# Routing weights spread by transfers from DRAM instead of by a selector product on TensorE

## What is computed

```
shared = silu(h @ Ws_up) @ Ws_down
biased = h @ centroids.T + expert_biases         # 64 experts; the 8 largest are chosen
w      = sigmoid of the 8 chosen affinities, divided by (their sum + 1e-8)
cw     = zeros(T, 64); cw[token, chosen] += w    # routing weights
y      = silu(h @ W_up[e]) @ W_down[e]           # 64 experts of 64 hidden units
x      = x + gb * (shared + sum over e of cw[:, e] * y[e])
```

## Time and profile before

| | us |
|---|---|
| median of 3 runs | 1983.4 |
| lowest, highest | 1980.77, 1983.73 |
| span of the profiled execution | 1978.2 |
| PE busy in the span | 1579.2 (80%) |
| DVE busy | 1410.5 (71%) |
| ACT busy | 1163.7 (59%) |
| POOL busy | 998.2 (50%) |

### The profile page before, as it was taken

How to read it: one execution, slowest core, us unless ns; L and a number is a source line. 1 busy time by engine, 2 the same in 40 slices (tenths; PEclk the granted TensorE clock), 3 DMA queues, 4 the chain that set the end, 5 groups by cost and what they waited for, 6 DMA issues and landing times. The chain is left out here.

```text
span 1978.2 us, 32338 instructions
## 1 busy us (share of the span) xinstructions
PE 1579.2 (80%) x9101; PEld 752.0 (38%) x9101; DVE 1410.5 (71%) x2630; ACT 1163.7 (59%) x1991; POOL 998.2 (50%) x923
## 2 busy tenths in 40 slices
PE   3599989898988889945764677777664999999998
PEld 2245444444444445422442122222222444444443
DVE  5677868686868687827766988898998555555554
ACT  1177766666667677625544444443333777777776
POOL 4144535353535353425862455544441667777776
PEclk7699989998999999976887777777777999999999
DMA  4332212131313131000003000000000000000000
GB/s 104 92 100 58 85 50 85 46 89 39 96 36 99 36 99 41 22 1 0 1 0 86 0 1 0 0 0 0 0 0 0 1 6 6 5 5 5 0 6 11
DMA packets 51217, 64.95 MB, mean 33 GB/s; under 512 B 7980, under 2 KB 42440, under 8 KB 51080
## 3 DMA queue, kind: packets, MB, share of 16 engines
q1 hardware_dynamic: 49640, 61.12, 10.8%
q10 hardware_dynamic: 1440, 2.10, 0.3%
HBM read 34.36 MB, written 28.05 MB: 32 GB/s over the span
## 5 line engine op out<-in xcount | busy, mean ns | idle before, releaser
L804 DVE TENSOR_REDUCE bmax<-p1b 128x4 f32<-128x512 f32 x640 | 408.5, 681 | 117.4 <-PE p1b L621 110.6
L553 ACT ACTIVATE pT<-p2b 128x512 f32<-128x512 f32 x640 | 373.2, 595 | 173.5 <-PE p2b L636 172.2
L1618 POOL TENSOR_TENSOR hid_l<-e_hid,hid_h 128x512 f16<-128x512 f32 x264 | 305.4, 1160 | 139.3 <-ACT hid_h L1758 138.2
L619 PE MATMUL p1b<-ks,qs 96*128 96x512 bf16 (+3 forms) x1024 | 274.0, 314 | 59.4 <-DVE bmax L804 33.0
L1864 DVE TENSOR_TENSOR e_hid<-act_u,e_cb 128x512 f32<-128x512 f32 x256 | 174.8, 687 | 187.6 <-ACT act_u L1772 163.5
L530 POOL TENSOR_SCALAR_AFFINE_SELECT pT<-pT 128x1280 f32<-128x1280 f32 (+2 forms) x192 | 162.3, 876 | 241.5 <-ACT pT L553 241.5
L636 PE MATMUL p2b<-qs,ks 96*128 96x512 bf16 (+3 forms) x1024 | 253.5, 310 | 7.3 <-ACT pT L553 6.7
L1772 ACT ACTIVATE act_u<-ub 128x512 f32<-128x512 f32 x264 | 157.3, 596 | 83.6 <-PE ub L1672 82.4
L621 PE MATMUL p1b<-causal,identb 128*128 128x128 bf16 x1024 | 200.1, 227 | 0.0
L649 PE MATMUL ob<-pT,vs 128*32 128x512 f32 (+3 forms) x2048 | 196.1, 456 | 2.2 <-POOL pT L530 2.2
L1479 DVE TENSOR_TENSOR_SCAN hs<-dA,dBx 128x512 f32<-128x512 f32 x128 | 183.3, 1432 | 17.0 <-ACT dA L1385 11.0
(11 more groups left out here) (254 smaller groups left out, 3027.5 us busy)
## 6 DMA issues: line engine op xcount, KB each, us to landing
qs<-q_stacks SPq DMA_DIRECT2D x64, 204.0 KB
q_stacks<-parts SPq DMA_DIRECT2D x96, 128.0 KB
k_stacks<-parts SPq DMA_DIRECT2D x96, 128.0 KB
ks<-k_stacks SPq DMA_DIRECT2D x64, 192.0 KB
qs<-nparts SPq DMA_DIRECT2D x192, 4.0 KB
out_dram<-x_tok SPq DMA_DIRECT2D x8, 256.0 KB, 2.3
wmod<-L_wmod SPq DMA_DIRECT2D x2, 384.0 KB, 5.8
q_stacks<-zeros SPq DMA_DIRECT2D x4, 192.0 KB, 3.1
```

Source lines behind the costliest of these rows:

```text
L553: act.activation(pT[:, g2 % 2, v, :], p2b[v % 2][:, :], ACT.Exp, scale=SCALE).then_inc(exp_done, 1)
L619: pe.matmul(bank[:, at * P:(at + c + 1) * P], qs[:, slot, m, c * P:(c + 1) * P], ks[:, slot, m, 0:(c + 1) * P], start=True, stop=False, sk ...
L804: dve.tensor_reduce(to, src, AX, ALU.max).then_inc(first_read, 1)
L1618: pool.tensor_tensor(hid_l[:, place(T), :], hid[:, place(T), :], hid_h[:, place(T), :], ALU.subtract).then_inc(split_ready, 1)
```

## The change

The selector and its matmul go. Once a batch the turned weights (64 x 512, f32, scaled by 64 on ACT) are stored to a DRAM tensor `shares`. For every slot SP then issues two transfers; each reads one row of 512 weights and writes it to 64 partitions of a tile of the ring `share` (eight tiles of 128x512 f32 in SBUF). DVE multiplies `act_u` with that tile. SP waits for `hid_ready` of the slot eight before, so that the tile is free. With the product go the two halves of the weights and what formed them: `double`, `high` and `split` become one activation `scaled_shares`, and the transpose reads `rest` itself. SP's program, which only stored the output before, is now a loop over rounds and slots. `share`, the function, is called `divide`.

```diff
-        pick = sb("e_pick", [P, ET, 2], FP16)
-        sel = sb("sel_e", [P, ET, P], FP16)
-        cw = sb("cw", [P, TILES, 2, E])
-        parts = sb("cw_parts", [P, 2, S], FP16)
-        low = sb("cw_low", [P, S])
+        turned_shares = sb("turned_shares", [E, S])
+        share = sb("share", [P, SHARES, S])
...
-            with sp.Fori(0, B) as r:
-                sp.wait_ge(x_ready, r + 2)
-                sp.dma_start(out[r, :, :].rearrange("(i p) d -> p i d", p=P), k.x[:, bass.ds(r * TILES, TILES), :]).then_inc(stored, 16)
+            def step(r, pre, main, post):
+
+                def save():
+                    b = r + 1
+                    sp.wait_ge(shares_ready, b + 2)
+                    sp.dma_start(shares_dram[b, :, :], turned_shares[:, :]).then_inc(shares_saved, 16)
...
+                if main:
+                    sp.wait_ge(shares_saved, (r + 1) * 16)
+                    for T in range(ET):
+                        before = T - SHARES if T >= SHARES else T - SHARES + ET - SLOTS
+                        if T >= SHARES or post:
+                            sp.wait_ge(hid_ready, r * SLOTS + before + 1 + RING)
+                        for a in range(2):
+                            sp.dma_start(share[a * EF:(a + 1) * EF, T % SHARES, :],
+                                         shares_dram[r, 2 * T + a, :].partition_broadcast(EF)).then_inc(share_loaded[T % SHARES], 16)
+                        if post and T == DOWN_LAG + SHARES + 4:
+                            store()
+                        if pre and T == ET - 2:
+                            save()
...
                 def turn_weights():
+                    pe.wait_ge(loaded, LOADS)
                     pe.wait_ge(cw_ready, b + 1)
                     for c in range(TILES):
-                        mm = pe.transpose(preb[:, c * P:(c + 1) * P], cw[:, c, :, :].rearrange("p a e -> p (a e)"), k.ident[:, :])
+                        mm = pe.transpose(preb[0:E, c * P:(c + 1) * P], rest[:, c, :], k.ident[:, :])
...
                 if main:
-                    pe.wait_ge(parts_ready, r + 3)
                     pe.wait_ge(hT_split, r + 1)
...
-                        if T < ET:
-                            pe.wait_ge(hid_ready, free(q, T, bank))
-                            pe.matmul(cb[bank(T)][:, :], sel[:, T, :], parts[:, r % 2, :], start=True, stop=True).then_inc(c_done, 1)
...
-                def high():
+                def scaled_shares():
                     act.wait_ge(cwT_done, b + 2)
-                    act.wait_ge(parts_ready, b + 2)
-                    act.activation(parts[:, b % 2, :], preb[:, :], ACT.Copy).then_inc(high_ready, 1)
+                    if main:
+                        act.wait_ge(shares_saved, b * 16)
+                    act.activation(turned_shares[:, :], preb[0:E, :], ACT.Copy, scale=W_SCALE).then_inc(shares_ready, 1)
...
                         if T < ET:
-                            dve.wait_ge(c_done, r * ET + T + 1)
-                            dve.tensor_tensor(hid[:, place(T), :], act_u[:, bank(T), :], cb[bank(T)][:, :], ALU.mult).then_inc(hid_ready, 1)
+                            dve.wait_ge(share_loaded[T % SHARES], (r * USES + T // SHARES + 1) * 32)
+                            dve.tensor_tensor(hid[:, place(T), :], act_u[:, bank(T), :], share[:, T % SHARES, :], ALU.mult).then_inc(hid_ready, 1)
```

More of the change, by code:

```diff
@@ L1515, in experts @@
     DOWN_LAG = 3
-    LOW = 2.0 ** 11
+    SHARES = 8
+    USES = ET // SHARES
+    shares_dram = nc.dram_tensor("shares", [B, E, S], F32).ap()
     with ExitStack() as ctx:
@@ L1547, in experts @@
         ub = [ps(f"ub{i}") for i in range(2)]
[L1548 removed]
         yb, preb, routeb, postb = ps("e_yb"), ps("e_preb"), ps("routeb"), ps("e_postb")
[L1550 removed]
+        share_loaded = [sem(f"share_loaded{s}") for s in range(SHARES)]
+        shares_saved = sem("shares_saved")
         cent_psum, cent_ready = sem("cent_psum"), sem("cent_ready")
[L1552 to L1554 removed]
+        xn_ready, xT_done, hT_ready, aff_done, sig_ready, cw_ready, cwT_done, shares_ready = (
+            sem("e_" + n) for n in ("xn_ready", "xT_done", "hT_ready", "aff_done", "sig_ready", "cw_ready", "cwT_done", "shares_ready"))
         biased_ready, top_ready, gate_ready = sem("biased_ready"), sem("top_ready"), sem("gate_ready")
[L1556 to L1557 removed]
+        u_done, silu_ready, hid_ready, hid_rounded, split_ready, down_done, yg_ready, turned, x_ready, hT_split = (
+            sem("e_" + n) for n in ("u_done", "silu_ready", "hid_ready", "hid_rounded", "split_ready", "down_done", "yg_ready",
                                     "turned", "x_ready", "hT_split"))
@@ L1561, in experts @@
         block = ctx.enter_context(nc.Block())
-        CREDITS = {silu_ready: RING, hid_ready: RING, split_ready: RING, down_done: RING, yg_ready: 1, turned: 1, x_ready: 1, parts_ready: 2, low_read: 1,
+        CREDITS = {silu_ready: RING, hid_ready: RING, split_ready: RING, down_done: RING, yg_ready: 1, turned: 1, x_ready: 1, shares_ready: 1,
                    biased_ready: 1, top_ready: 1, aff_done: 1, cwT_done: 1}
@@ L1590, in _, with store @@
         def _(sp):
-            with sp.Fori(0, B) as r:
-                sp.wait_ge(x_ready, r + 2)
-                sp.dma_start(out[r, :, :].rearrange("(i p) d -> p i d", p=P), k.x[:, bass.ds(r * TILES, TILES), :]).then_inc(stored, 16)
+            def step(r, pre, main, post):
[3 more added lines that the diff above has]
+                    sp.dma_start(shares_dram[b, :, :], turned_shares[:, :]).then_inc(shares_saved, 16)
+                def store():
+                    sp.wait_ge(x_ready, r + 1)
+                    sp.dma_start(out[r - 1, :, :].rearrange("(i p) d -> p i d", p=P), k.x[:, bass.ds((r - 1) * TILES, TILES), :]).then_inc(stored, 16)
+                if main:
[11 more added lines that the diff above has]
+                            save()
+                elif pre:
+                    save()
+                else:
+                    store()
+            rounds(sp, step)
             sp.wait_ge(stored, B * 16)
@@ L1599, in _ @@
                 pool.sem_inc(s, n)
[L1600 to L1607, removed]
             def step(r, pre, main, post):
@@ L1777, in step @@
                         if pre:
-                            for at, f in ((4, pre_h), (10, sigmoid), (21, high)):
+                            for at, f in ((4, pre_h), (10, sigmoid), (21, scaled_shares)):
                                 if T == at:
@@ L1781, in step @@
                 elif pre:
-                    pre_h(), sigmoid(), high()
+                    pre_h(), sigmoid(), scaled_shares()
                 else:
@@ L1818, in strike @@
                 def strike():
-                    dve.wait_ge(loaded, LOADS)
+                    dve.wait_ge(cwT_done, b + 1)
                     dve.wait_ge(top_ready, b + 2)
+                    dve.sem_inc(passed, 1)
                     for c in range(TILES):
@@ L1835, in total, with divide @@
                     link(dve.reciprocal(wsum[:, :], wsum[:, :]))
[L1837 to L1842, removed]
-                steps = ((0, pre_norm), (9, bias), (10, largest), (11, strike), (12, mask), (13, chosen), (14, total), (15, share), (16, double))
-                def split():
-                    dve.wait_ge(high_ready, b + 1)
-                    lo = parts[E:2 * E, b % 2, :]
-                    dve.tensor_tensor(low[E:2 * E, :], preb[E:2 * E, :], lo, ALU.subtract).then_inc(low_read, 1)
-                    dve.wait_ge(low_read, b + 2)
-                    dve.tensor_scalar(lo, low[E:2 * E, :], LOW, None, ALU.mult).then_inc(parts_ready, 1)
+                def divide():
+                    dve.tensor_tensor(rest[:, :, :], rest[:, :, :], wsum[:, :].unsqueeze(2).broadcast_to([P, TILES, E]), ALU.mult).then_inc(cw_ready, 1)
+                steps = ((0, pre_norm), (9, bias), (10, largest), (11, strike), (12, mask), (13, chosen), (14, total), (15, divide))
                 def residual():
@@ L1869, in step @@
                         if pre:
-                            for at, f in (*steps, (21, split)):
+                            for at, f in steps:
                                 if T == at:
```

10 lines of the change are left out of this document (2 added, 8 removed).

## The result

The changed kernel takes **1998.0 us** (median of four executions, 1994.5 to 2001.2). The kernel before, on the same chips, takes 1982.1 (four executions, 1978.8 to 1983.7). The ratio is 1.0089, with an interval of 1.007 to 1.0107: the change costs some 16 us. The profiled span grew from 1978.2 to 1996.7, by 18.5 us.

The account below looks back on a forecast made before the run. TensorE bounded the old kernel (1.51 us a slot); GpSimd and VectorE in turns (1.56) the new. Span 1978.2 + 7.7 (rounds) + 1.9 (start) + 1.6 (end) = 1989, plus 5.2 to the median: 1994 us, range 1970 to 2035.

Parts of the forecast that it names:

- rival C: Expert slots: full lengths of product and subtraction exclude each other, 1.85 us a slot, about 2067 us; chance 0.06.
- term (a): Start of a round: each normalisation waits its turn, products 1 to 3 come late, turns resume 1.2 us late.
- term (b): ScalarE's switch to sigmoid and back, some 4.3 us, partly filled by turns and hT: 0.8 us lost a round.
- term (c): Routing steps in a round push GpSimd a slot ahead, costing 0.5 us.
- B: Expert slots: exclusion hardly bites, ScalarE bounds at 1.22 us a slot, round 49 us, about 1935 us; chance 0.09.
- G: Rounds: turns rule but the gaps nearly vanish, round 53.9 us, total 1974 us; chance 0.10.
- D: SP and transfers too slow, VectorE waits for every pair: 2076 us, mild form 2000 to 2030; chance 0.08.
- E: TensorE's gaps of 0.3 us per slot bring its clock to 1.2 GHz, 2.6 us a slot; chance 0.02.
- (1): VectorE's product: mean well over 0.69 us, about 1.4, since it stands in its turn, never under.
- (4): Rounds between gated results take 56 to 57 us.
- (5): TensorE is busy about 10 points less, its clock still 1.00.
- (6): VectorE's waits on share transfers are near zero save in round 0.

Follow-up runs that it names:

- e1: Changed kernel with its transfers, but VectorE's product reads a constant PSUM tile instead of the share tile (routing weights left out): 1947.3 us, ratio 0.9832.
- e3: Kernel before with its seven matmuls, no transfers, but the product reads a constant SBUF tile instead of bank e_cb (weights left out): 2012.4 us, ratio 1.0156.
- e4: Changed kernel with silu's result act_u in the two freed PSUM banks, complete computation: 1946.1 us, ratio 0.982.
- e2: Changed kernel without the save, loads and waits of the weights; share tiles filled once with ones: 1996.0 us, ratio 1.0064.
- e5: Changed kernel with VectorE's strike halved after slots 11 and 12, mask to divide a slot later: 1994.3 us, ratio 1.0079.
- e7: The unaltered changed kernel timed again, as reference beside the halved strike: 1999.1 us, ratio 1.0102.

## Why the prediction was right

The forecast was 1994, in a range of 1970 to 2035, with "slower" at 0.66; it came out at 1998.0, slower. Its likeliest case is the one that happened, and e1, e3 and e4 show its cause.

**The slot.** 0.54 + 1.02 = 1.56 us from three pairs of the earlier trace rows; measured 1.56 (0.56 + 1.00). The sum is right to the hundredth because its two parts are off by 0.02 in opposite ways (the earlier trace rows themselves give 0.55 for the first). The full lengths (rival C, 1.85) are refuted in nearly every slot. The Trainium skill (SBUF — State Buffer, section "SBUF: two separate sides") says that whoever starts first holds the port pair for the whole instruction. The turns agree with it; "the whole instruction" does not, since in each turn some 0.14 us of the instruction lies beside the other's (0.69 less 0.56, 1.16 less 1.00). Which part of the instruction that is, as "before the first read" in the prediction, no row shows.

**The gaps of a round** were the term that was mis-sized. A round took 57.6, not 56.5. The forecast's gaps beyond the turns were 2.5 us, and 3.7 came. Its terms can be held against the ends of the products. Slots 0 to 5: six turns, 0.8 for the normalisations and term (a) make 11.4; measured 11.44. Slots 10 and 11, across ScalarE's switch: two turns, 1.0 for hT and term (b) make 4.9; measured 4.99. Slots 12 to 18: seven turns, 0.8 for the routing operations and term (c), 0.5 us for "the routing steps push GpSimd a slot ahead", make 12.2; measured 13.3. So term (c) was 1.1 us a round too small. The missing time first shows at the strike, behind which the product ended 2.69 after the one before and not 1.56, since GpSimd was 0.03 us ahead. With another order of turns e2 gets back 0.8 of it and e5 0.6. The table under e4 adds what the forecast does not say. Against the kernel before, the 0.05 us per slot matters little (0.2 in slots 20 to 32, and slots 0 to 10 even take 0.7 less). The round is 2.2 us longer because slots 11 to 19, where VectorE's routing steps join the turns, take 2.7 us more.

**The parts of the sum.** Up to the first gated result I had 1.9 for the start and 1.1 for round 0, 3.0; measured 4.4. The wait for the first transfer was right within 0.3 (2.2). What I left out is that TensorE, having stood, is at the low clock later than before. The delay grows by 0.9 us over those slots (in e7 too), and the six matmuls shown above, at the low clock, take 1.28 us more; no run isolates it. The rest of round 0 took 1.3, where 1.1 was forecast. Five whole rounds: 5.5 forecast, 11.1 measured, nearly all of the difference from term (c). From the last gated result on: 1.1 for a round and 1.6 for the end, 2.7; measured 3.0. There the sum hides an error: one round's 2.2 is in it, which leaves 0.7 for the last round without routing, not 1.6.

**The carry-over to the median** was wrong the other way. I added to the forecast span the 5.2 us by which the median of before lay above its profiled span. After, the median is 1.3 above the span (1998.0 against 1996.7), and that profiled execution itself was timed at 1998.4, 1.7 above its span. So most of the 5.2 was that one execution of before being short of its median. The span was underrated by 8 us, the median by 4, and part of the accuracy is luck.

**The rivals.** B (no exclusion, 1935) is what e1 and e4 build on purpose, and its price was 12 us too low. It named ScalarE as the bound at 1.22 us a slot, although the prediction's own 6 x 0.216 = 1.29 for TensorE is more; the bound there is TensorE with 1.30, and the extras are 8.3 us, not what the earlier trace rows suggested. G (gaps vanish) is refuted by the rounds of 57.6, 3.7 of them gaps. D is refuted by the waits and by e2. E has a grain of truth only in round 0. That nobody else waits on SP was misread: ScalarE waits for the save of the batch before (`shares_saved`), but no such wait shows in the trace.

**The marks.** (1) Product well over 0.69: 1.25 on average and 1.49 in the slots shown; 1.4 was asked for, the average holds products that nobody disturbed. (2) Subtraction over 1.16: 1.48. (3) Turns of 1.56: as said. (4) Rounds of 56 to 57: 57.6, just outside, for the reason above. (5) TensorE 10 points less: 9, clock 0.98. (6) Waits on transfers: 0.8 us beyond the first slots.

## What to carry to other kernels

Before an operand of VectorE moves from PSUM to SBUF, look at what GpSimd does at that time: two neighbouring operations whose ends alternate at fixed distances are taking turns, and their turns add up to a bound that no engine's share of busy time shows. The edit that frees PSUM also holds the remedy: give one of the two operands a freed bank (here ScalarE's result, 1998 to 1946 us). And where two engines take turns, a step that holds one of them away for some 1 us can change the order of turns for several slots (here 0.6 to 0.8 us a round), so its place is worth a look, but only as long as the turns are there.

## What the runs showed of the hardware that I had not expected

A difference of 0.01 to 0.03 us in who starts first decides who stands, and with the order of turns behind it 0.8 us a round. It repeats in all rounds of the changed kernel (also in e7) and falls the other way in all rounds of a nearly equal one (e2). In e5 the order is not the same in each round, and rounds of one program take 56.8 to 57.7 us. The strike's replacing steps, which take 64 columns of one SBUF tile (the eight values are loaded by a step ahead), take 0.21 us beside a running subtraction on GpSimd, which is not stretched by them either (1.15 us): the two do not exclude each other there, where a product of two tiles would. ScalarE's silu into PSUM takes 0.58 us, against 0.60 into SBUF. And 128 KB broadcasts at 174 GB/s, over half of all the DMA engines' time in e4, did not slow any engine's operation on SBUF that I could see.
